# A two-layer transformer kernel on one Trainium2 core: one more group's output by seven block products

## The reference, cut to what matters

```python
attn_out = softmax(x@Wq @ (x@Wk).T * scale) @ (x@Wv) @ Wp + bp
cms_out  = gelu(attn_out @ cW1 + cb1) @ cW2 + cb2 + one_hot(codes)
modifier = gelu(concat([attn_out, cms_out]) @ mW1 + mb1) @ mW2 + mb2
y        = clip(x + cms_out + modifier, 0, 1)
out      = layernorm(y + gelu(y @ W_down[s] + b_down[s]) @ W_up[s] + b_up[s]) * ln_w[s] + ln_b[s]
```

## Time and profile before

| | |
|---|---|
| time, median of 3 runs | 1068.65 us (1065.85 to 1068.96) |
| the profiled execution | 1067.02 us, span 1065.2 us |
| mean granted clock of TensorE | 0.998 |
| busy PE / DVE / POOL / ACT | 1050.2 / 717.7 / 584.9 / 474.2 us |

### The profile page before, as it was taken

One profiled execution on the slowest core, in us unless ns is written; L12 is line 12 of the kernel. 1 busy time (PEld: TensorE's weight loads), 2 busy tenths in 40 slices (PEclk: granted clock), 3 DMA queues, 4 the chain that ended last, 5 costly groups with the idle time before them and its releaser, 6 DMA issues.

```text
span 1065.2 us, 13654 instructions
## 1 busy us (share of the span) xinstructions
PE 1050.2 (99%) x4675; PEld 867.4 (81%) x4675; DVE 717.7 (67%) x1020; ACT 474.2 (45%) x901; POOL 584.9 (55%) x577
## 2 busy tenths in 40 slices
PE   9999999999999999999998999999998999999998
PEld 7888888888888888888886888888886888888786
DVE  4735353396466555555786888885787888887768
ACT  3645345454333334333543443444543444333765
POOL 0575774532232331430888766776896666673406
PEclk9999999999999999999999999999999999999999
DMA  7455630101223322111043443435846434335834
GB/s 277 143 171 192 227 109 5 56 0 46 74 74 104 120 74 95 49 35 55 25 173 124 124 133 120 129 109 165 329 174 202 134 119 119 108 110 180 315 80 158
DMA packets 88212, 134.10 MB, mean 126 GB/s; under 512 B 7376, under 2 KB 53200, under 8 KB 87632
## 3 DMA queue, kind: packets, MB, share of 16 engines
q1 hardware_dynamic: 87568, 132.18, 37.4%
q10 hardware_dynamic: 576, 1.05, 0.3%
HBM read 98.34 MB, written 34.87 MB: 125 GB/s over the span
## 4 chain that ended last, share of the span: by engine, by line
PE 91%; DVE 2%; POOL 2%; DMA 2%; issue 2%; ACT 0%; SPq 0%; ACTq 0%; DVEq 0%; POOLq 0%
PE bank L914 30%; PE bank L916 30%; PE bank L915 30%; DMA up_lo<-experts_split 1%; DMA y_kept<-acc 1%; PE bank L1137 1%; PE bank L971 1%; DMA acc<-xT_dram 1%; POOL c_B_lo L714 1%; DVE c_T_f L1565 1%; DVE acc L1642 0%; DVE H_lo L1617 0%; PE bank L940 0%; POOL c_T_lo L714 0%; POOL left_x L714 0%
## 5 line engine op out<-in xcount | busy, mean ns | idle before, releaser
L714 POOL TENSOR_TENSOR left_x<-rawX,left_x 128x256 fp32r<-128x256 f32 x144 | 133.2, 926 | 160.9 <-ACT left_x L1199 160.9
L1642 DVE TENSOR_TENSOR acc<-bank,acc 128x512 f32<-128x512 f32 x136 | 92.0, 687 | 49.9 <-PE bank L916 49.3
L914 PE MATMUL bank<-H_hi,W_hi 128*128 128x512 f32 x304 | 118.3, 389 | 0.0
L916 PE MATMUL bank<-H_hi,W_lo 128*128 128x512 f32 x304 | 118.3, 389 | 0.0
L915 PE MATMUL bank<-H_lo,W_hi 128*128 128x512 f32 x304 | 118.3, 389 | 0.0
L1701 DVE TENSOR_TENSOR acc<-bank,acc 128x512 f32<-128x512 f32 x166 | 107.2, 684 | 8.3 <-PE bank L916 4.7
L914 PE MATMUL bank<-x_T_hi,left_x 128*128 128x512 f32 x256 | 100.1, 391 | 0.0
L916 PE MATMUL bank<-x_T_hi,left_x 128*128 128x512 f32 x256 | 100.1, 391 | 0.0
L915 PE MATMUL bank<-x_T_lo,left_x 128*128 128x512 f32 x256 | 100.1, 391 | 0.0
L1631 DVE TENSOR_TENSOR u_t<-bank,s_t 128x512 f32<-128x512 f32 x64 | 44.2, 690 | 82.2 <-PE bank L916 78.3
L714 POOL TENSOR_TENSOR left_c<-rawC,left_c 128x256 fp32r<-128x256 f32 x96 | 90.4, 942 | 1.0 <-ACT left_c L1199 1.0
(11 more groups left out here) (224 smaller groups left out, 2816.7 us busy)
## 6 DMA issues: line engine op xcount, KB each, us to landing
ring<-w_kept SPq DMA_DIRECT2D x91, 256.0 KB, 2.7
rawX<-mW_dram SPq DMA_DIRECT2D x16, 512.0 KB, 3.9
rawC<-mW_dram SPq DMA_DIRECT2D x16, 512.0 KB, 4.9
w_kept<-mod_hi SPq DMA_DIRECT2D x7, 896.0 KB, 4.4
w_kept<-mod_lo SPq DMA_DIRECT2D x7, 896.0 KB, 7.3
xT_raw<-xT_dram SPq DMA_DIRECT2D x4, 1024.0 KB, 8.6
x_raw<-x_dram SPq DMA_DIRECT2D x4, 1024.0 KB, 6.1
rawX<-cW_dram SPq DMA_DIRECT2D x8, 512.0 KB, 3.7
```

The lines of the kernel that those rows point to most:

```text
L714: pool.tensor_tensor(dst, src, f32(hi), ALU.subtract).then_inc(done, 1)
L914: pe.matmul(tile, sh, mh, start=first_one and n == 0, stop=False, skip_group_check=joined_group)
L916: last = pe.matmul(tile, sl, mh, start=False, stop=last_one and n == len(terms) - 1, skip_group_check=joined_group)
L1642: op = dve.tensor_tensor(dst, src, dst, ALU.add)
```

## The change

Group 22 is computed in the SEVEN form, so the first run of such groups is 16 to 22, one longer, and FOUR holds 23 and 31. The first run then has seven groups like the second, and the ring's buffers are dealt out by one rule. What stood in the loop's own code for group 23 (sums T1, T2, T4, the split of T2, the late `join` of C12) is written into `seven_group` for g = 23. The splitting of group 23's second matrix by ACT leaves the middle of group 23 and falls under the rule for a FOUR group behind a SEVEN one: load after steps 1 and 4, split at the start of the next group.

```diff
--- before.py
+++ after.py
@@ -311,7 +311,7 @@
 
 
 
-        RUNS = (range(16, 22), range(24, 31))
+        RUNS = (range(16, 23), range(24, 31))
         SEVEN = [g for run in RUNS for g in run]
         FOUR = [g for g in range(MOD0, GROUPS) if g not in SEVEN]
         tiles_ahead = [8 * g + 6 * len([q for q in SEVEN if q < g]) for g in range(GROUPS)]
@@ -355,7 +355,7 @@
                 if g < run[-1]:
                     k = n % 4
                 else:
-                    k = ((3, 2, 0, 1, 3, 0, 1) if n - j == 35 else (2, 3, 0, 1, 2, 0, 1))[j]
+                    k = (2, 3, 0, 1, 2, 0, 1)[j]
                 ring_uses[k] += 1
                 ring_of[g, j] = k, ring_uses[k]
                 ring_next.setdefault(had.get(k, run[0] - 1), []).append((g, j))
@@ -1411,8 +1411,6 @@
                 gelu(g, C22)
                 if g == 23:
                     co_hi(1, T2)
-                if g == 23:
-                    second_hi(second_set(g))
                 gelu(g, C21)
                 if g == MOD0:
                     left_hi(*splits_in(g)[1], 1, g)
@@ -1738,11 +1736,17 @@
                 gelu_low(g, C11)
                 add_staged(g, step(p, 3, 1))
                 add_step(p, 4)
+                if g == 23:
+                    for op in (T1, T2, T4):
+                        co_sum(1, op)
                 join(g, JC21)
                 gelu_low(g, C22)
                 add_step(p, 5)
-                join(g, JC12)
+                if g != 23:
+                    join(g, JC12)
                 add_step(p, 6)
+                if g == 23:
+                    co_lo(1, T2)
 
             dve.wait_ge(bias_step, 2 + B)
             for g in range(GROUPS):
```

## The result

The changed kernel takes **1081.84 us** (median of 3 runs, 1080.76 to 1082.32) against 1068.65: ratio 1.0132, 95% interval 1.0119 to 1.0146. The profiled execution took 1082.32, with a span of 1080.5 and a mean granted clock of 0.992.

The account below looks back on a forecast made before the run. PE, busy 99% of the span, was taken as the bound. -1.4 + 11.0 + 5.0 + 3.0 - 1.7 = +15.9, taken as +15, gave 1082 us for the profiled execution and 1083.5 for the median, range 1077 to 1088.5.

Parts of the forecast that it names:

- The two waits: PE idle before step 6 in group 23 (+11.0 us) and before the first W_hi matmul in group 24 (+5.0 us).
- all the signs put down for them: PE idle 7 to 12.5 us before step 6, 2 to 5 before W_hi; DVE idle 5 to 8; half clock after.
- The first rival: Only the copies count: group 23's W_lo is ready in time because PE runs slow; 1079 us, chance 0.14.
- Part 1: Group 22's output needs 14 products of three matmuls in place of 16, six matmuls fewer: -1.36 us.
- Part 2: Group 23: four copies queue behind W_raw's load, so DVE's three sums and then step 6 come late: +11.0 us.
- The prediction's second way: Landing of the four copies: W_raw's landing at 755.3 plus 1.27 us per 512 KB copy, giving 760.3.
- its rival of the hidden wait: Last copy landed by 750 leaves only -1.4 us, 1067.3; chance 0.04 within 0.3%, 0.02 faster.
- Part 3: Group 23's second matrix: the later join of C12 delays W_lo, so PE waits before W_hi: +5.0 us at full clock.
- the collision: W_lo on POOL takes 3.4 us, as c_B_lo did beside DVE's sums, in place of 2.39.
- Part 4: PE's clock falls to half after both waits: 1.3 us through step 6, 1.7 after the second; +3.0, bounds 0 and 5.
- Part 5: Group 25: the first idle piece, 1.67 us, vanishes and the second stays: -1.7 us, bounds 0 and -5.
- an overlap: Parts 3 and 4 overlap a little more than could be resolved, so +15.9 us was taken as +15.

Follow-up runs that it names:

- run 6: Changed kernel with SP issuing the x copies only when the four c copies have landed: 1081.81 us, ratio 1.0138 to the kernel before.
- run 1: Changed kernel with the four copies of the second pair's sums issued ahead of the reloads that wait for group 22's steps: 1075.29 us, ratio 1.0070.
- Run 2: Changed kernel with the join of C12 in its usual place, ahead of the addition of step 6: 1079.05 us, ratio 1.0107.
- run 7: Changed kernel with both edits of run 3, the three sums set apart, and POOL's first c_B_lo held until H_lo of C22 is made: 1071.40 us, 1.0039.
- run 9: Run 7 without POOL's hold, so its subtraction for B11 may start once the first sum is made: 1070.35 us, ratio 1.0024.
- run 10: Run 9 with the sum T4 moved behind the addition of step 6: 1068.15 us, ratio 1.0008.
- run 11: Run 10 with POOL's split W_lo ahead of the adapter's piece and the last splits of the first matrix: 1068.57 us, ratio 1.0015.
- run 5: Changed kernel with 48 matmuls whose results nobody reads on PE, in the wait ahead of step 6: 1081.50 us, ratio 1.0133.
- run 3: Changed kernel with both edits, copies issued early and the join of C12 in its usual place: 1072.02 us, ratio 1.0042.
- run 4: Changed kernel with POOL's c_B_lo waiting for DVE's third sum in place of the first: 1081.76 us, ratio 1.0140.
- run 8: Kernel before, group 22 in its old form, with its four c copies waiting for product T3 of group 23 in place of B11: 1074.56 us, 1.0069.
- run 12: Run 11 with group 25's clip ahead of sums V, T3, T4 and the save ahead of the first matrix's loads: 1066.00 us, ratio 0.9987.

## Why the prediction was right, step by step

1083.5 was forecast with a range of 1077 to 1088.5; measured were 1081.84. The two waits, their places and their releasers were as written, and all the signs put down for them came. The first rival, W_lo ready in time, is ruled out by the 4.37 us of waiting for it. That the number fits so well is in part luck, as the sum at the end shows.

**Part 1** (-1.36): the counts differ by six; nothing ahead of the two waits shows another cost.

**Part 2** (+11.0, measured +11.56). Less the 0.74 by which all ran earlier, W_raw was forecast for 750.72 and was issued then; the four copies for 751.2 to 752.7, measured 751.15 to 752.68. The rows of one group, moved on, gave the queue to within a few hundredths. The landing was forecast for 760.3; it came at 760.9, and DVE began at 761.06. Sums 5.76 for 5.8, pair and handover 2.02 for 2.14. The prediction's second way, W_raw's landing and 1.27 us for each copy, gives 759.6 here. That it came 1.3 us later is for the most part not the work of the copies behind: run 6, with none behind, still took 7.6 us, which would be 760.3. So the second way's price for the four copies was too low, and the 5.9 to 9.0 us of the old copies were the better guide. The Trainium skill (DMA: Bandwidth & Descriptors, "Queues, rings and completion order") says that descriptors are consumed in ring order on each DMA engine. That copies issued behind then take nothing from those ahead was the prediction's own reading; run 6 puts it at 0.3 to 0.6 us. Run 1 showed what the prediction had wrong beside this: its rival of the hidden wait said that with the copies landed by 750 only the -1.4 would be left. In run 1 they had landed by 745, and 3.7 of the 11 us stayed, because three sums of 1.2 us beside POOL's subtraction take 5.8 and stand ahead of an addition that PE waits for.

**Part 3** (+5.0, with the clock's 1.3 in front of it 6.3; measured 6.33). The join of C12 stood 5.28 us behind step 6's start, forecast 4.5 at full clock and 5.8 at half; W_lo took 3.33, near the 3.4 of the collision. Run 2 shows that without the join's new place there is no such wait in the changed kernel. Runs 7, 9, 10 and 11 show a second limit behind it: once DVE is on time, POOL's backlog sets W_lo.

**Part 4** (+3.0; about +2.2). The clock fell as written. Behind step 6 the slow matmuls only shortened the next wait, as written; for the chain through step 6 I had 1.3, and with a busy PE (run 5) it was 0.5 shorter. The 1.7 behind the second wait are in the windows (0.68, then 0.50).

**Part 5** (-1.7, measured -3.9, inside its bounds of 0 to -5). This is the term that was mis-sized. The first idle piece vanished as written: DVE waited 0.22 us for the gelu in place of 4.29. The second piece was to end with a copy into acc and keep its distance; it fell from 2.05 to 0.33. The copy acc<-xT_dram was issued 14.0 us later than before (807.31, then 821.28), PE came 15.7 later, and so the data were there in time: DVE waited 2.98 us for PE and not for them. The low clock behind the two pieces went too (-1.7). Against this stands the new piece of 1.23 ahead of step 6. One of 0.96 to 1.52 us stands there in all nine traces in which the clock stays full in group 25 (the changed kernel, runs 1, 3 to 7, 9 and 10) and in none of the five in which it falls (the kernel before, runs 2, 8, 11 and 12).

**The sum** was right by errors that cancelled: 2.2 too little back in group 25 and a start 0.74 earlier on one side, 0.6 in part 2 and 1.6 of small waits behind it that were not forecast on the other. The 0.9 that was taken off the +15.9 for an overlap has no measured counterpart of its own. The profiled execution was forecast at 1082 and took 1082.32; the 1.5 us added for the median were not there, since its distance from the median is chance.

## What to carry to other kernels

A list that one queue works through turns "one more wait ahead of it" into lateness of all that stands behind: look for copies that stand behind a new wait, and issue them ahead of it (7.7 us of PE's waiting and 6.5 us of the time here). On an engine at 99%, what is gained is only kept if the next fixed chain is not due there: look after each repair where the idle time comes back, and follow that wait to the copy or the order that sets it (run 11, then 12). A saving of 1.4 us that re-times the boundary between two stages is to be costed by that boundary, which took six further edits to put in order.

## What the runs showed of the hardware

- An operation of DVE with two operands in SBUF took longer where it met a subtraction of POOL on 128x1024: a pair of sums 4.51 us in place of 2.55, with POOL's subtraction at 3.39 in place of 2.35 (the changed kernel against run 4), and in run 4 DVE's next subtraction 2.52 in place of 0.68, while POOL's kept its 2.35. Delaying one only moved the loss.
- An idle time of the same length need not have the same effect on the clock. 3.69 us ahead of step 6 in run 1 brought a low clock of 6.8 us, 3.68 us there in run 3 none. Long ahead of the change PE is idle for 2.17 to 2.20 us in all fourteen traces, until 570.4 to 571.4, and the clock fell behind it in eight and stayed full in six. A window of the kernel before, then of the changed kernel:

```profile
571.00:573.00 2.00, 2.00 (x9) 1.61 (x9) 0.34 (x1) 0.42 (x1) 1.47 (x2) 1.00 1.02 327
```

```profile
571.00:573.00 2.00, 2.00 (x7) 1.53 (x6) 0.09 (x1) 0.41 (x2) 1.41 (x3) 0.52 1.02 366
573.00:575.00 2.00, 2.00 (x7) 1.58 (x6) 1.03 (x2) 0.93 (x2) 2.00 (x3) 0.63 0.70 203
```

- Such a low clock, 3.4 us at half, need not cost the 1.7 us of PE's work that are lost in it. From the end of that idle time to the first matmul of group 23 the eight traces with it take 159.4 to 159.8 us, the six without it 159.2 to 160.0: those six have two more waits there, of 0.3 to 1.0 us (until about 576) and 0.6 us (until about 586), which the other eight lack. It is as with the piece ahead of step 6 in group 25. Why the clock falls in one execution and not in the next stays open.
- How long the low clock lasts does not follow from the idle time either: 10 us with 11.4 of idle time, 3.4 with 4.4 (the changed kernel), 3.4 and 2.8 (runs 11 and 10), but 6.8 with 3.7 and again with 3.5 (run 1). That PE is put to 1.2 GHz when idle agrees with the Trainium skill (TensorE: Matmul & The Clock Gate, Part 1) for the idle time of 11.4 us; behind the 3.68 us of run 3 it was not.
